# Decoder on one core: the last routed down product in three rounded products, and causal attention's sums transposed between two pairs of pieces

## Chip, cores, metric

One Trainium2 chip, one of its cores, the whole decoder in one launch. The metric is the device time of the execution in microseconds; lower is better. Runs are compared by their median.

## The reference

Four decoder layers over x of 2 x 1024 tokens of 256 values, each with self-attention (or a recurrence), cross-attention to a context of 77 tokens, and a feed-forward, each followed by x = layernorm(x + part(x)). Two parts matter here.

Layer 1's self-attention is causal, with 16 heads of 16 values. Layer 3's feed-forward is routed: 16 experts, 4 per token.

```python
logits = hidden_states @ router_w + router_b
probs = jax.nn.softmax(logits, axis=-1)
topw, topi = jax.lax.top_k(probs, K)                 # K = 4, E = 16
topw = topw / jnp.sum(topw, axis=-1, keepdims=True)
...
hmid = jax.nn.gelu(x @ w1e + b1e, approximate=False) # 256 -> 512
return (acc + (hmid @ w2e + b2e) * ce[:, None], None)  # 512 -> 256
```

## The kernel before

Each engine has its own program, written out by hand; semaphores order them, and every engine works through its own instructions in order. `wait_ge(s, n)` waits until a semaphore has counted to n.

**The routed feed-forward** (`routed_moe`, L2805) is used twice: for layer 1 with a gated unit (`glu`), and last of all for layer 3 without one, which the code calls `biased`. Tokens are sorted by expert into NBLK = 79 blocks of TB = 128 rows. For block j:

- SP (L2930) loads the expert's weights, 1026 KB, into one of WB = 6 buffers `w` as soon as the down product of block j-6 is done. POOL (L2967) gathers the rows into `xb` 6 blocks ahead (`fetch`) and stores the result `yb` to DRAM when it is kept.
- TensorE (L3005): `spin(j)` transposes the rows (L3069), `lift(j)` makes the hidden block in PSUM tiles `A` (8 products of 128x128 by 128 columns, L3082), `drop(j)` the down product in `C` (4 products of 256 columns, L3090). A product of full float32 operands shows as two records in the trace. The order is spin(j+1), lift(j), drop(j-1), and for blocks 2 to 17 also `settle(j-2)` (L3062), gates times bias.
- ACT (L3139): `turn(j+1)` copies the transposed rows (L3155), then four Gelus (L3178) make `hid`. In the last four blocks it also makes the gate diagonals that the final sums need, 8 copies a block (L3195).
- DVE (L3220): `hold(j-1)` copies the down product out of PSUM into `yb` (L3326), and settle's part adds x (L3314).

`C` has two banks. `order` (L2827) deals them out: through drop 16 the drops and the settle products alternate, so that all drops take one bank and drop(j) needs hold(j-1); later the drops alternate and drop(j) needs hold(j-2).

Behind the last block, the results are read back, weighted by the gates, summed, normalised and stored.

**Causal attention** (`stacked_attention`, L1146, `kind` "causal"; the same function with "full" does layer 2). Two things run at once: the row maxima of a later head group, computed in "pieces" that TensorE puts into a ring of 3 PSUM banks (L1491) and DVE reduces (L1632, L1636), and the softmax of the present group: scores `st_ps` (L1483), exponentials on ACT (L1616), and the weighing with the values into the bank `acc` (L1530). When half a group of heads is done ("closing"), DVE transposes the sums from `acc` into `byq` (L1674) and inverts them (L1676); the next half's first weighing waits for `turned`. There are 16 such closings. One step of TensorE is: scores of pair 0 with pieces 2 and 3, weigh (first half of the columns), scores of pair 1 with pieces 0 and 1, weigh (second half, if any), extras. The closing step of a causal half has 128 columns, which all go into the first weigh.

Products in float32r ("rounded") take operands that ACT or DVE has rounded on writing; a float32 value is split into a rounded high part and the rounded rest, and three products (high by high, high by low, low by high) stand for one. The kernel does this already in layer 0's and layer 2's feed-forwards: `hid_hi` L1095, `hid_lo` L1097, `x_hi` and `x_lo` L1071 and L1085, and the products of L2673.

Of the kernel before, what the change touches and what calls it, by code (L numbers as in the profile page):

```python
# [5 lines left out]
F32 = mybir.dt.float32  # L6
F32R = mybir.dt.float32r
# [4 lines left out]
ALU = mybir.AluOpType  # L12
# [3 lines left out]
P = 128  # L16
D = 256
# [1128 lines left out]
def stacked_attention(nc, env, dram, kind, scale, w_count, front, ahead=None):  # L1146
# [86 lines left out]
    with ExitStack() as st:  # L1233
# [3 lines left out]
        with ExitStack() as inner:  # L1237
# [384 lines left out]
            def _(dve):  # L1622
# [55 lines left out]
                def put(step):  # L1678
                    g, half = step // nS, half_of[step % nS]
                    b, u = units[g]  # L1680
                    if u % 2:
                        dve.wait_ge(s.divided, g * HALVES + half + 1)
                        dve.transpose(o[:, u // 2, b * S + half * CH:b * S + (half + 1) * CH], pair[:, half, :]).then_inc(s.evacuated, 1)
# [9 lines left out]
                for step in range(NS + LAG + 3):  # L1693
                    c = step + LEAD if step + LEAD < NC else None
                    if c is not None:
                        pieces(c, (2, 3))
                    if closing(step - LAG - 2):
                        put(step - LAG - 2)
                    if c is not None:
                        pieces(c, (0, 1))  # L1700
                    if closing(step - LAG):
                        turned(step - LAG)
                    if c is not None:
                        extras(c)
# [1100 lines left out]
def routed_moe(nc, env, dram, E, K, F, glu, shared, out=None, ahead=None, front=None, early=None):  # L2805
# [25 lines left out]
    with ExitStack() as st:  # L2831
        z = sbuf(nc, st, "z", [P, NT, D])
        b2 = sbuf(nc, st, "b2", [E, D])
        sc = sbuf(nc, st, "sc", [P, NT, E])
        rowmax = sbuf(nc, st, "rowmax", [P, NT])
        top = sbuf(nc, st, "top", [P, NT, 8])
        topi = sbuf(nc, st, "topi", [P, NT, 8], U32)
        total = sbuf(nc, st, "total", [P, NT])
        g = sbuf(nc, st, "g", [P, NT, K])
        idf = sbuf(nc, st, "idf", [P, NT, K])  # L2840
        eq = sbuf(nc, st, "eq", [P, NT, K, E])
        prod = sbuf(nc, st, "prod", [P, NT, K, E])
        sel = sbuf(nc, st, "sel", [P, E, NT])
        fresh = sbuf(nc, st, "fresh", [P, E, NT])
# [24 lines left out]
        dense = sbuf(nc, st, "dense", [P, NT, E])  # L2869
        gT = sbuf(nc, st, "gT", [E, T])  # L2870
        w = early.w if early else sbuf(nc, st, "w", [P, WB, ROW])
        xb = sbuf(nc, st, "xb", [P, XB, D])
        xbT = sbuf(nc, st, "xbT", [P, 2, KT, TB])
        if front:
            act, hid = (r.rearrange("p a b s -> p (a b s)").rearrange("p (x f n) -> p x f n", x=2, f=NF)
                        for r in (front.parts[:, :, :, :].bitcast(F32), front.plain[:, :, :, :]))
        else:
            act, hid = None, sbuf(nc, st, "hid", [P, 2, NF, TB])
        yb = sbuf(nc, st, "yb", [P, 4, D])
        room = sbuf(nc, st, "room", [P, RU * PAIR * K * D])  # L2880
        stat = sbuf(nc, st, "stat", [P, NT, 6])
        mv = sbuf(nc, st, "mv", [P, NT, 2])
# [8 lines left out]
            for at, n, k in ((0, TB, K), (K * TB, NBLK, K), (K * (TB + NBLK), NBLK, K),  # L2891
# [5 lines left out]
                     "lists_ready owner_ready dense_ready gT_ready gT_kept z_ready z_added s_up s_act s_hid "  # L2897
                     "w0 w1 w2 w3 w4 w5 x0 x1 x2 x3 x4 x5 x6 x7 t_ready t_kept up_ready act_ready "
                     "hid_ready down_done y_kept stored0 stored1 stored2 stored3 got0 got1 got2 got3 got4 got5 got6 got7 "
                     "g_ready scaled blended mixed measured rooted inverted shifted normed spun kept out_stored")  # L2900
        w_ready = (s.w0, s.w1, s.w2, s.w3, s.w4, s.w5)
        x_ready = (s.x0, s.x1, s.x2, s.x3, s.x4, s.x5, s.x6, s.x7)
        stored = (s.stored0, s.stored1, s.stored2, s.stored3)
# [22 lines left out]
        def down_w(src_w, f):  # L2926
            at = NW * KT * F + f * D
            return src_w[:, at:at + D]

        @block.sync  # L2930
        def _(sp):
# [74 lines left out]
        def _(pe):  # L3006
# [65 lines left out]
            def lift(j):  # L3072
# [10 lines left out]
                                           start=(k == 0), stop=(k == KT - 1), skip_group_check=True)  # L3083
                mm.then_inc(s.up_ready, 1)

            def drop(j):
                pe.wait_ge(s.hid_ready, j + 1)
                to = room_c(("drop", j))
                for f in range(NF):
                    mm = pe.matmul(to, hid[:, j % 2, f, 0:TB], down_w(w[:, j % WB], f),  # L3090
                                   start=(f == 0), stop=(f == NF - 1))
                mm.then_inc(s.down_done, 1)
# [47 lines left out]
        def _(act_e):  # L3140
# [16 lines left out]
            def keep(u):  # L3157
                for t in range(u * PAIR, (u + 1) * PAIR):
                    act_e.wait_ge(s.spun, t + 1)
                    act_e.activation(env.xT[:, :, t * P:(t + 1) * P], B[:, t % 2, 0:D].rearrange("p (k n) -> p k n", k=KT), ACT.Copy)\  # L3160
                         .then_inc(s.kept, 1)

            turn(0)
            for j in range(NBLK):
                if j + 1 < NBLK:
# [7 lines left out]
                    act_e.activation(act[:, j % 2, :, 0:TB], A[:, j % 2 * 2, :].rearrange("p (f n) -> p f n", f=NF), ACT.Silu).then_inc(s.act_ready, 1)  # L3173
                else:
                    if j >= 2:
                        act_e.wait_ge(s.down_done, j - 1)
                    for f in range(NF):
                        a = act_e.activation(hid[:, j % 2, f, 0:TB], A[:, j % 2 * 2, f * TB:(f + 1) * TB], ACT.Gelu,  # L3178
                                             bias=w[:, j % WB, NWE + f:NWE + f + 1])
                    a.then_inc(s.hid_ready, 1)  # L3180
                    if j < 2:
                        act_e.wait_ge(s.gT_ready, j + 1)
                        for a in range(2):
                            at = j * (T // 2) + a * CH
                            kept = act_e.activation(gT[:, at:at + CH], A[0:E, 1 + 2 * a, :], ACT.Copy)
                        kept.then_inc(s.gT_kept, 1)
# [34 lines left out]
        def _(dve):  # L3221
# [100 lines left out]
            def hold(j):  # L3322
# [2 lines left out]
                    dve.wait_ge(stored[j % 4], 16 * (j // 4))  # L3325
                dve.tensor_copy(yb[:, j % 4, :], C[:, spot[("drop", j)] % 2, 0:D]).then_inc(s.y_kept, 1)  # L3326

            for j in range(NBLK):
                if glu:
                    dve.wait_ge(s.act_ready, j + 1)  # L3330
                    if j >= 2:
                        dve.wait_ge(s.down_done, j - 1)
                    dve.tensor_tensor(hid[:, j % 2, :, 0:TB], act[:, j % 2, :, 0:TB],  # L3333
                                      A[:, j % 2 * 2 + 1, :].rearrange("p (f n) -> p f n", f=NF), ALU.mult).then_inc(s.hid_ready, 1)
                if j:
                    hold(j - 1)
                    if biased and 0 <= j - 2 < NT:
                        settle(j - 2)
# [311 lines left out]
```

## Time and profile before

| | us |
|---|---|
| median of 3 runs (2590.24 to 2604.8) | 2594.25 |
| the profiled execution's own time | 2600.38 |
| its span, first to last instruction | 2598.6 |
| TensorE products busy, of the span | 2276.5 |
| VectorE busy | 1431.6 |
| ScalarE busy | 1125.8 |
| GpSimd busy | 659.1 |

The mean granted TensorE clock is 0.908 of full speed. PE is TensorE's matmul, PEld its weight load, DVE VectorE, ACT ScalarE, POOL GpSimd, SP the engine that issues most transfers. A row of the timeline merges equal instructions that follow each other; "[0.43 <-PE ring L1491]" is idle time ahead of it and what ended that. Matmuls overlap in the pipeline, so their rate is read from start to start, not from the duration of one.

### The profile page before, as it was taken

Reading aid. Unit: us, or ns where it says so; the run is one execution under the profiler, and the core shown is the slowest. Engines: PE = TensorE matmul, PEld = TensorE weight load, DVE = VectorE, ACT = ScalarE, POOL = GpSimd, SP = SyncE. Lnnn points to the kernel's source line nnn. Section 1 sums busy time; section 2 is a strip of 40 time slices with the busy share of each in tenths; the row PEclk is TensorE's granted clock in tenths of the full one; section 3 lists DMA queues with packets and bytes.
Section 4 is the critical chain, followed back from the end, with each engine's and each line's share of the span. In section 5 each row is a group of like instructions: output and inputs, shape, how many; then the busy total and the mean of one; then the engine's idle time right before and its main releaser. Section 6 shows DMA issues by size and latency. Waiting matters only on the chain. (4 is left out here: it accounts for less than half of the span.)

```text
span 2598.6 us, 41898 instructions
## 1 busy us (share of the span) xinstructions
PE 2276.5 (88%) x15210; PEld 1512.3 (58%) x15210; DVE 1431.6 (55%) x3533; ACT 1125.8 (43%) x1923; POOL 659.1 (25%) x868
## 2 busy tenths in 40 slices
PE   1489999998889999949999998799998798699996
PEld 1387754444436699934444444367665545589995
DVE  6825366785565221158999965666566555511114
ACT  6533335655433011134777774421443334234444
POOL 6110132222110133322011012000356310245551
PEclk8689978988998999966999999789999898699998
DMA  5200122330112189933222101031111210689996
GB/s 195 64 5 1 27 48 46 50 50 18 30 34 106 39 309 334 329 108 54 34 41 35 26 7 46 2 91 58 33 27 19 57 18 2 217 293 354 355 343 235
DMA packets 86208, 268.89 MB, mean 103 GB/s; under 512 B 25306, under 2 KB 43858, under 8 KB 69740
## 3 DMA queue, kind: packets, MB, share of 16 engines
q1 hardware_dynamic: 70324, 233.10, 29.4%
q0 software_dynamic: 15680, 33.12, 4.0%
q8 instruction: 122, 2.00, 0.3%
q14 instruction: 82, 0.67, 0.1%
HBM read 207.36 MB, written 23.94 MB: 89 GB/s over the span
## 5 line engine op out<-in xcount | busy, mean ns | idle before, releaser
L1616 ACT ACTIVATE prob<-st_ps 128x1024 f32<-128x1024 f32 x448 | 412.9, 933 | 220.0 <-PE st_ps L1483 218.7
L1636 DVE TENSOR_REDUCE cmax<-ring 128x1 f32<-128x512 f32 x640 | 401.2, 682 | 43.7 <-PE ring L1491 41.4
L3082 PE MATMUL A<-xbT,w 128*128 128x128 f32 x2512 | 301.3, 276 | 0.3 <-issue 0.3
L3082 PEld LDWEIGHTS A<-xbT,w 128*128 128x128 f32 x2512 | 291.4, 193 | 0.8 <-issue 0.5
L1530 PE MATMUL acc<-prob,v 128*32 128x256 f32 (+2 forms) x3200 | 267.0, 408 | 13.4 <-DVE byq L1674 12.3
L3326 DVE COPY yb<-C 128x256 f32<-128x256 f32 x118 | 50.1, 425 | 283.7 <-PE C L3090 277.5
L2999 POOL DMA_INDIRECT y_rows_dram<-yb,dst x118 | 116.4, 986 | 323.8 <-DVE yb L3326 320.7
L3090 PE MATMUL C<-w,hid 128*128 128x256 f32 x632 | 149.5, 380 | 0.0
L1483 PE MATMUL st_ps<-qst,kst 64*128 64x512 f32 (+3 forms) x560 | 137.3, 489 | 7.3 <-DMA qst<-parts 3.1
L2986 POOL DMA_INDIRECT xb<-x_rows_dram,src x118 | 115.1, 976 | 99.9 <-DVE src L3296 64.6
L1632 DVE CUSTOM_DVE_ANT_0 masked<-ring,causal_wide 128x512 bf16<-128x512 f32 (+3 forms) x256 | 112.5, 487 | 47.8 <-PE ring L1491 46.9
L3178 ACT ACTIVATE hid<-A,w 128x128 f32<-128x128 f32 x316 | 90.3, 369 | 105.6 <-PE A L3082 102.8
L1530 PEld LDWEIGHTS acc<-prob,v 128*32 128x32 f32 x3200 | 65.2, 110 | 120.7 <-issue 104.2
L1491 PE MATMUL ring<-kst,qst 48*128 48x512 f32 (+3 forms) x560 | 127.4, 402 | 2.4 <-DVE cmax L1632 1.8
L1483 PEld LDWEIGHTS st_ps<-qst,kst 64*128 64x128 f32 x560 | 54.9, 192 | 115.3 <-issue 77.9
L3090 PEld LDWEIGHTS C<-w,hid 128*128 128x128 f32 x632 | 114.0, 190 | 12.5 <-ACT hid L3178 0.3
L3155 ACT ACTIVATE xbT<-B 128x256 f32<-128x256 f32 x118 | 45.2, 384 | 171.0 <-PE B L3069 168.6
L1491 PE MATMUL ring<-first 48*128 48x512 f32 (+3 forms) x336 | 106.5, 490 | 10.7 <-PEq L3458 7.4
L2468 ACT ACTIVATE prob<-st_ps 77x1024 f32<-77x1024 f32 x64 | 61.8, 1015 | 124.5 <-PE st_ps L2382 68.0
L2352 PE MATMUL max_ps<-kbd,qT 128*128 128x308 f32 x320 | 109.4, 440 | 5.2 <-DVE negc L2479 3.8
L3333 DVE TENSOR_TENSOR plain<-parts,A 128x512 f32<-128x512 f32 x39 | 26.9, 689 | 155.7 <-ACT parts L3173 155.7
L2479 DVE TENSOR_REDUCE negc<-max_ps 128x4 f32<-128x308 f32 x160 | 76.0, 478 | 60.0 <-PE max_ps L2356 47.2
(475 smaller groups left out, 4491.7 us busy)
## 6 DMA issues: line engine op xcount, KB each, us to landing
w<-L3f_W_dram SPq DMA_DIRECT2D x79, 1026.0 KB
w<-L1f_W_dram SPq DMA_DIRECT2D x39, 1536.0 KB
room<-y_rows_dram SPq DMA_DIRECT2D x8, 1024.0 KB, 10.4
kst<-parts SPq DMA_DIRECT2D x120, 64.0 KB, 2.4
qst<-parts SPq DMA_DIRECT2D x120, 64.0 KB, 2.4
gate<-L2f_gates_dram SPq DMA_DIRECT2D x5, 1536.0 KB, 7.1
first<-parts SPq DMA_DIRECT2D x96, 64.0 KB, 2.4
qT<-dense SPq DMA_DIRECT2D x84, 64.0 KB, 2.4
```

The costliest lines, as they stand in the source:

```text
L1483: mm = pe.matmul(st_ps[:, p, side, 0:hi - lo], stack_of(1, g)[rows, p, j * P:(j + 1) * P], stack_of(0, g)[rows, p, lo:hi], start=True, sto ...
L1491: pe.matmul(spot(key)[:, 0:k1 - k0], stack_of(0, gm)[rows, 1 - p, t * P:(t + 1) * P], stack_of(1, gm)[rows, 1 - p, k0:k1], start=True, sto ...
L1530: mm = pe.matmul(acc[32 * a:32 * (a + 1), lo - half * CH + c0:lo - half * CH + c1], v[:, g // 2 % 2, j, units[g][1] % 2 * HU + a, :], prob ...
L1616: act.activation(prob[:, step % PROBS, 2 * p:2 * p + 2, 0:n], st_ps[:, p, :, 0:n], ACT.Exp, scale=scale)\
L1632: dve.tensor_tensor_reduce(out=masked[:, a, 0:k1 - k0], in0=spot(key)[:, 0:k1 - k0], in1=env.causal_wide[:, CH - (k1 - k0):], scale=1.0, s ...
L1636: dve.tensor_reduce(cmax[:, a, t:t + 1, k0 // CH], spot(key)[:, 0:k1 - k0], AX.X, ALU.max)\
L2352: mm = pe.matmul(to, qT[:, g % SLOTS, t * P:(t + 1) * P], kbd[:, u, b].rearrange("p a m -> p (a m)"), start=True, stop=(not masked), skip_ ...
L2986: pool.indirect_dma_start(out=xb[:, j % XB, :], out_offset=None, in_=rows[:, :], in_offset=bass.IndirectOffsetOnAxis(ap=src[:, j:j + 1], a ...
L2999: pool.indirect_dma_start(out=yk, out_offset=bass.IndirectOffsetOnAxis(ap=dst[:, j:j + 1], axis=0), in_=yb[:, j % 4, :], in_offset=None).t ...
L3082: mm = pe.matmul(A[:, j % 2 * 2 + a, f * TB:(f + 1) * TB], up_w(w[:, j % WB], a, k, f), xbT[:, j % 2, k, :], start=(k == 0), stop=(k == KT ...
L3090: mm = pe.matmul(to, hid[:, j % 2, f, 0:TB], down_w(w[:, j % WB], f), start=(f == 0), stop=(f == NF - 1))
L3178: a = act_e.activation(hid[:, j % 2, f, 0:TB], A[:, j % 2 * 2, f * TB:(f + 1) * TB], ACT.Gelu, bias=w[:, j % WB, NWE + f:NWE + f + 1])
```

## The change

In `stacked_attention`, for causal attention alone, DVE does `turned` (wait for the closing weigh, transpose, reciprocal) between the pieces 2, 3 and the pieces 0, 1 of a step, instead of behind both.

In `routed_moe`, for the last feed-forward alone: ACT rounds each block's down weights (`raise_down`, once ahead of the loop and then behind the Gelus of the block before); DVE subtracts to get their low part (`lower_down`) and splits the hidden block (`part_hid`), ahead of `hold`; `drop` becomes 12 rounded products. Its Gelu waits for the split of block j-2, no longer for its drop. To make room for the four new buffers, `sc` and `eq` are laid into `env.wide`, and `xb`, `yb` and `hid` into `env.xT`.

```diff
                     if closing(step - LAG - 2):
                         put(step - LAG - 2)
+                    if kind == "causal" and closing(step - LAG):
+                        turned(step - LAG)
                     if c is not None:
                         pieces(c, (0, 1))
-                    if closing(step - LAG):
+                    if kind == "full" and closing(step - LAG):
                         turned(step - LAG)
...
+            def drop_in_parts(j):
+                pe.wait_ge(s.down_low, j + 1)
+                pe.wait_ge(s.hid_low, j + 1)
+                to = room_c(("drop", j))
+                for f in range(NF):
+                    cols = slice(f * D, (f + 1) * D)
+                    pe.matmul(to, hid_hi[:, j % 2, f, :], down_hi[:, j % 2, cols], start=(f == 0), stop=False)
+                    pe.matmul(to, hid_hi[:, j % 2, f, :], down_lo[:, j % 2, cols], start=False, stop=False)
+                    mm = pe.matmul(to, hid_lo[:, j % 2, f, :], down_hi[:, j % 2, cols], start=False, stop=(f == NF - 1))
+                mm.then_inc(s.down_done, 1)
+
             def drop(j):
+                if biased:
+                    drop_in_parts(j)
+                    return
                 pe.wait_ge(s.hid_ready, j + 1)
...
+            def raise_down(j):
+                act_e.wait_ge(w_ready[j % WB], 16 * (j // WB + 1))
+                if j >= 2:
+                    act_e.wait_ge(s.down_done, j - 1)
+                act_e.activation(down_hi[:, j % 2, :], down_rows(j), ACT.Copy).then_inc(s.down_high, 1)
+
+            if biased:
+                raise_down(0)
             turn(0)
...
                     if j >= 2:
-                        act_e.wait_ge(s.down_done, j - 1)
+                        act_e.wait_ge(s.hid_low, j - 1)
                     for f in range(NF):
                         a = act_e.activation(hid[:, j % 2, f, 0:TB], A[:, j % 2 * 2, f * TB:(f + 1) * TB], ACT.Gelu,
                                              bias=w[:, j % WB, NWE + f:NWE + f + 1])
                     a.then_inc(s.hid_ready, 1)
+                    if j + 1 < NBLK:
+                        raise_down(j + 1)
...
+            def lower_down(j):
+                dve.wait_ge(s.down_high, j + 1)
+                dve.tensor_tensor(down_lo[:, j % 2, :], down_rows(j), down_hi[:, j % 2, :].bitcast(F32), ALU.subtract).then_inc(s.down_low, 1)
+
+            def part_hid(j):
+                dve.wait_ge(s.hid_ready, j + 1)
+                if j >= 2:
+                    dve.wait_ge(s.down_done, j - 1)
+                dve.tensor_copy(hid_hi[:, j % 2], hid[:, j % 2]).then_inc(s.hid_high, 1)
+                dve.wait_ge(s.hid_high, j + 1)
+                dve.tensor_tensor(hid_lo[:, j % 2], hid[:, j % 2], hid_hi[:, j % 2].bitcast(F32), ALU.subtract).then_inc(s.hid_low, 1)
+
+            if biased:
+                lower_down(0)
             for j in range(NBLK):
+                if biased:
+                    part_hid(j)
+                    if j + 1 < NBLK:
+                        lower_down(j + 1)
```

## Rows read from the trace of the kernel before

**Rows 1.** Stretches: us, busy us of PE, PEld, DVE, ACT, POOL, granted clock, DMA share, GB/s

```profile
2230.00:2240.00 10.00, 9.93 (x63) 8.49 (x61) 7.22 (x9) 0.00 (x0) 0.00 (x0) 0.50 0.99 411
2262.00:2322.00 60.00, 60.00 (x372) 49.15 (x371) 11.04 (x26) 21.01 (x69) 25.68 (x27) 1.00 0.88 294
2340.00:2530.00 190.00, 190.00 (x1325) 176.97 (x1323) 21.65 (x51) 77.91 (x255) 99.48 (x102) 1.00 0.96 351
```

**Rows 2.** The timeline, one block (start us, us, engine, line, operation, count)

```profile
2402.37 1.95 PE L3082 MATMUL A<-xbT,w 128*128 128x128 f32 x16
...
2404.15 1.89 PE L3090 MATMUL C<-w,hid 128*128 128x256 f32 x8
...
2404.36 1.15 ACT L3178 ACTIVATE hid<-A,w 128x128 f32<-128x128 f32 x4 [1.40 <-PE A L3082]
...
2405.88 0.38 PE L3069 MATMUL B<-ident,xb 128*128 128x128 f32 x2
...
2406.09 0.42 DVE L3326 COPY yb<-C 128x256 f32<-128x256 f32 x1 [3.31 <-PE C L3090]
2406.10 1.95 PE L3082 MATMUL A<-xbT,w 128*128 128x128 f32 x16
2406.30 0.38 ACT L3155 ACTIVATE xbT<-B 128x256 f32<-128x256 f32 x1 [0.80 <-PE B L3069]
```

**Rows 3.** The timeline of TensorE, two drops among the early blocks

```profile
2270.84 1.89 PE L3090 MATMUL C<-w,hid 128*128 128x256 f32 x8
...
2275.35 1.89 PE L3090 MATMUL C<-w,hid 128*128 128x256 f32 x8
```

**Rows 4.** The waits in causal attention: us in total, times, longest

```profile
PE acc L1530 <- DVE byq L1674: 1.6, 4, 0.4
```

**Rows 5.** The timeline of TensorE, the first and last of nine rounded products, dense feed-forward

```profile
1724.12 0.39 PE L2673 MATMUL hid_ps<-x_hi,w_hi 128*128 128x512 f32 x1
...
1725.99 0.40 PE L2673 MATMUL hid_ps<-x_hi,w_lo 128*128 128x512 f32 x1
```

**Rows 6.** The timeline, pairs of half-height rounded products, 256 and 512 columns

```profile
478.53 0.39 PE L1483 MATMUL st_ps<-first 64*128 64x256 f32 x2
...
478.75 0.53 PE L1491 MATMUL ring<-kst,qst 48*128 48x512 f32 x2
...
530.31 0.50 PE L1483 MATMUL st_ps<-qst,kst 64*128 64x512 f32 x2
530.65 0.79 PE L1491 MATMUL ring<-kst,qst 48*128 48x512 f32 x2
```

**Rows 7.** The groups of instructions by line before 340 us (busy us, mean ns | idle before)

```profile
L1097 DVE TENSOR_TENSOR hid_lo<-lift,hid_hi 128x512 fp32r<-128x512 f32 x32 | 22.1, 692 | 1.1
...
L1095 DVE CAST hid_hi<-lift 128x512 fp32r<-128x512 f32 x32 | 13.7, 429 | 10.1 <-ACT lift L1077 10.1
...
L1085 DVE TENSOR_TENSOR first<-xT,parts 128x1024 fp32r<-128x1024 f32 x4 | 4.6, 1221 | 6.0 <-ACT parts L1071 6.0
...
L1071 ACT ACTIVATE parts<-xT 128x1024 fp32r<-128x1024 f32 x4 | 3.9, 1045 | 1.3 <-PEq L3423 1.3
```

**Rows 8.** The timeline, the last four blocks

```profile
2542.52 1.14 ACT L3178 ACTIVATE hid<-A,w 128x128 f32<-128x128 f32 x4 [1.40 <-PE A L3082]
...
2544.31 2.45 ACT L3195 ACTIVATE w<-ident,g 128x128 f32<-128x128 f32 x8 [0.65 <-PE C L3090]
...
2553.30 3.75 PE L3090 MATMUL C<-w,hid 128*128 128x256 f32 x16
```

**Rows 9.** The timeline, one closing in causal attention

```profile
477.55 0.43 PE L1530 MATMUL acc<-prob,v 128*32 128x128 f32 x8
...
478.44 0.29 DVE L1632 CUSTOM_DVE_ANT_0 masked<-ring,causal_wide 128x128 bf16<-128x128 f32 x1 [0.43 <-PE ring L1491]
...
478.87 0.71 DVE L1674 STREAM_TRANSPOSE byq<-acc 128x512 f32<-128x512 f32 x1
...
479.73 0.64 PE L1530 MATMUL acc<-prob,v 128*32 128x256 f32 x8 [0.44 <-DVE byq L1674]
```

More of the change, by code:

```diff
@@ L2833, in routed_moe @@
         b2 = sbuf(nc, st, "b2", [E, D])
-        sc = sbuf(nc, st, "sc", [P, NT, E])
+        sc = env.wide[:, 4 * KT * P:4 * KT * P + NT * E].rearrange("p (t e) -> p t e", t=NT) if biased else sbuf(nc, st, "sc", [P, NT, E])
         rowmax = sbuf(nc, st, "rowmax", [P, NT])
@@ L2840, in routed_moe @@
         idf = sbuf(nc, st, "idf", [P, NT, K])
-        eq = sbuf(nc, st, "eq", [P, NT, K, E])
+        eq = env.wide[:, 0:NT * K * E].rearrange("p (t k e) -> p t k e", t=NT, k=K) if biased else sbuf(nc, st, "eq", [P, NT, K, E])
         prod = sbuf(nc, st, "prod", [P, NT, K, E])
@@ L2871, in routed_moe @@
         w = early.w if early else sbuf(nc, st, "w", [P, WB, ROW])
-        xb = sbuf(nc, st, "xb", [P, XB, D])
+        flat_xT = env.xT[:, :, :].rearrange("p k t -> p (k t)")
+        xb = flat_xT[:, 0:XB * D].rearrange("p (x d) -> p x d", x=XB) if biased else sbuf(nc, st, "xb", [P, XB, D])
         xbT = sbuf(nc, st, "xbT", [P, 2, KT, TB])
@@ L2877, in routed_moe @@
         else:
-            act, hid = None, sbuf(nc, st, "hid", [P, 2, NF, TB])
-        yb = sbuf(nc, st, "yb", [P, 4, D])
+            act, hid = None, flat_xT[:, (XB + 4) * D:(XB + 4) * D + 2 * NF * TB].rearrange("p (x f n) -> p x f n", x=2, f=NF)
+            hid_hi = sbuf(nc, st, "hid_hi", [P, 2, NF, TB], F32R)
+            hid_lo = sbuf(nc, st, "hid_lo", [P, 2, NF, TB], F32R)
+            down_hi = sbuf(nc, st, "down_hi", [P, 2, NF * D], F32R)
+            down_lo = sbuf(nc, st, "down_lo", [P, 2, NF * D], F32R)
+        yb = flat_xT[:, XB * D:(XB + 4) * D].rearrange("p (x d) -> p x d", x=4) if biased else sbuf(nc, st, "yb", [P, 4, D])
         room = sbuf(nc, st, "room", [P, RU * PAIR * K * D])
@@ L2899, in routed_moe @@
                      "hid_ready down_done y_kept stored0 stored1 stored2 stored3 got0 got1 got2 got3 got4 got5 got6 got7 "
-                     "g_ready scaled blended mixed measured rooted inverted shifted normed spun kept out_stored")
+                     "down_high down_low hid_high hid_low g_ready scaled blended mixed measured rooted inverted shifted normed spun kept out_stored")
         w_ready = (s.w0, s.w1, s.w2, s.w3, s.w4, s.w5)
@@ L2928, in down_w, with down_rows @@
             return src_w[:, at:at + D]
+        def down_rows(j):
+            return w[:, j % WB, NW * KT * F:NWE]
         @block.sync
```

## The prediction

> **What bounds the kernel now.** I read the busy time by stretch first, then one block of the last stage in the timeline, then the same for the causal closings. The last stage, the routed feed-forward with 79 blocks, takes the last 350 us but the final sums. In it TensorE has no idle time at the 2.4 GHz level (granted clock 1.00), once 190 us long at 351 GB/s and a DMA share of 0.96 [rows 1]. The timeline of a block shows why: lift, down product ("drop") and transposes ("spin") follow each other without a gap, lift 2402.37 to 2404.15 = 1.78 us, drop to 2405.88 = 1.73, spin to 2406.10 = 0.22, together 3.73 us, while ACT waits for the lift and DVE for the drop [rows 2]. In the blocks up to about 17, which also have a gate-times-bias product, the period is 2275.35 - 2270.84 = 4.51 us [rows 3]. So TensorE sets this stage, and the DMA queues have little left. In causal attention a head group closes 16 times; the next accumulation there waits for the transpose of the sums only 1.6 us in all, 4 times [rows 4].
>
> **The drop.** It loses 4 full products (8 records, 1.73 us) and gets 12 rounded ones of 256 columns. The trace has none of that shape with all 128 rows. Nearest: nine rounded products of 512 columns start between 1724.12 and 1725.99, 1.87 / 8 = 0.234 us apart, each with a weight load of its own [rows 5]; by column that is 0.457 ns, so 0.117 us for 256. The pairs of half-height rounded products take 0.22 us for 256 columns and 0.34 for 512 [rows 6]: 0.12 more for 256 more columns, so the same rate, on a base of 0.10 us that looks like an exposed weight load. Lower bound 0.111: lift's 16 records, which move two passes of 128 columns and load 128 weight columns each, take 1.78 us [rows 2]. Upper bound 0.22. I take 0.117, because the full-height row is nearest in form: 12 x 0.117 = 1.40 us, 0.33 less. TensorE's block would then be 3.40 us.
>
> The Trainium skill (TensorE: Matmul & The Clock Gate, Part 3, The mechanism) says that a weight load overlaps running matmuls only when its row group differs, which would put a full-height product at load plus stream. By that rule the drop would take 12 x 0.22 = 2.6 us; the full-height rows disagree, as 16 loads and 16 products fit in 1.78 us [rows 2].
>
> **What ACT and DVE get.** Per block ACT rounds the down weights, 128x1024: 1.05 us by the like copy; DVE subtracts them, 1.22, rounds the hidden block, 0.43, and subtracts, 0.69 [rows 7]. ACT has then 0.38 + 1.15 + 1.05 = 2.58 us a block and DVE 1.22 + 0.43 + 0.69 + 0.42 = 2.76, both under 3.40 [rows 2, 7]. The order matters. Gelu starts with the end of lift(j) and takes 1.15; the two hidden parts are ready 1.15 + 0.43 + 0.69 = 2.3 us behind it, 2.4 with handovers; drop(j) comes only after drop(j-1), spin and lift(j+1), 1.40 + 0.22 + 1.78 = 3.4 us. Hidden, with 1.0 us to spare; without that cover the drop would wait by the difference.
>
> The copy-out of drop(j-1) now stands on DVE behind the parts of block j and the low weights of block j+1, and those wait for ACT, which waits for drop(j-1). From the start of drop(j-1): 1.40 + 0.17 (its last product's tail: 2404.15 + 1.89 against 2405.88) + 1.05 + 1.22 + 0.42, with four handovers of some 0.04, 4.4 us. Up to block 17 the drops share one PSUM bank, so drop(j) waits for just this copy: period 4.4, not 4.51 - 0.33 = 4.18. Gain 17 x 0.1 = 2 us. Behind, two banks alternate and the wait has a period to spare. The gathers and stores on POOL move later by some 2.3 us but run 6 blocks ahead and 4 buffers deep; the weights of block j+6 are issued by SP at the same event as before, the end of drop(j). The rounding of block j+1 waits on ACT for that block's transfer and for drop(j-1), with turn(j+2) queued behind it; lift(j+1) needs the same transfer and turn(j+2) is wanted a block later: nothing. Moving xb, yb, hid, sc and eq into other memory adds no instruction; nothing else of the last stage uses that memory.
>
> **DMA.** At 351 GB/s a 3.73 us block moves 1.31 MB. The engines' time per block is share times period: 0.96 x 3.73 = 3.58 us; in the slower early blocks it is 0.88 x 4.51 = 3.97 [rows 1, 3]. It falls by half of what the period falls; carried on, it meets the period at 3.43, and if it falls no more, at 3.58. A block between 3.40 and 3.58: I take the middle, 3.49, 0.24 less than now, over the 58 blocks from 17 to 75: 14 us. What is late then is the weight transfer in flight.
>
> **The end.** In the last four blocks ACT also makes the gate diagonals, 2.45 us each. With the weights' rounding its turn is 0.38 + 1.15 + 1.05 + 2.45 = 5.03 us, above 3.4, so it sets the pace. From the first of these Gelus at 2542.52 to the last product's end at 2553.30 + 3.75 the trace has 14.5 us [rows 8]. New: three ACT turns of 5.03, 0.4 in which the first rounding waits for drop(74), less 0.38 for the turn that the last lacks, Gelu 1.15, parts 1.12, handovers, drop 1.40 + 0.17: 19.1 us. Loss 4.6. The first weights' rounding lies under the wait for the lists: nothing.
>
> **Causal closings.** The closing step's weighing ends at 477.55 + 0.43 = 477.98, ahead of the pieces for which DVE waits 0.43 us until 478.44; the transpose starts only at 478.87, and the product that needs it at 479.73 after 0.44 us [rows 9]. Moved, the transpose (0.71) and the small reciprocal run from 478.0 to about 479.0, and the two pieces follow 0.5 us later than before; their ring places come free later, and TensorE's next pieces wait. Each event lies between 0.44 won and 0.5 lost: over 16, -7 to +8 us. As DVE's idle 0.43 is used but the ring takes most of it back, I take 1 us won.
>
> **Sum.** 14 + 2 - 4.6 + 1 = 12.4 us. The profiled execution (2598.6 us of span, 2600.4 in all) would be 2588. It is 6 us above the median of the three runs, 2594.25, and of that I forecast 2582.
>
> **Rivals.**
> - DMA keeps its pace. The 351 GB/s over 190 us may be the ceiling of this mix of weights, gathers and stores; then a block stays at 3.73 and the end still costs: 0 + 2 - 4.6 + 1, 2 us lost, 2596. For: share 0.96. Against: weight transfers alone ran at 411 GB/s [rows 1]. The Trainium skill (DMA: Bandwidth & Descriptors, Specifications) puts HBM's limit for one core at about 358 GB/s, which is 1.31 / 358 = 3.66 us a block and 2592 for the whole; the 411 GB/s disagree.
> - Weight loads exposed, the slow side. As in the pairs [rows 6], each rounded product costs 0.22: drop 2.64, 0.91 more than now. 58 x 0.91, 17 blocks of 3.0 + 2.64 against 4.51 (19 us), the end at 4.6 + 1.2, less 1: 77 us, 2671. It decides early: at 0.136 a product the gain is gone, at 0.15 the kernel is over 0.5% slower. For: the 0.10 us base in the pairs. Against: the full-height rows [rows 5].
> - TensorE alone sets the block. DMA follows to 3.40: 19 + 2 - 4.6 + 1 = 17 us, 2577; with the closings at their best 2571.
> - The closings turn bad: the pieces' ring stalls TensorE at every closing, 8 us back, 2591. DVE's wait on the sums then stands in front of work that had been ready.
>
> **How the numbers follow.** Measured against the median, 0.5% (13 us) is about what can be told from no change. Forecast 0.38, with its block between 3.43 and 3.58 (2579 to 2587); TensorE alone 0.29; DMA's pace 0.14; closings bad 0.08; exposed loads 0.11. Faster by over 0.5%: TensorE alone and two fifths of the forecast, 0.44. Slower: exposed loads and a little for causal attention, 0.13. The same: 0.43. The range goes from 2569, closings won besides, to 2602, closings bad with DMA at its pace and a few us between runs; beyond it lie the exposed loads.
>
> **What would show it.** Right: 12 down records 0.117 us apart at full clock; blocks of about 3.5 us with a DMA share near 1.0 and lift waiting on the weights' transfer now and then; 4.4 us before block 17 with drop waiting for yb; ACT without a gap in the last four blocks, the drops there waiting for hid_lo; in causal attention the transposes about 0.9 us earlier, DVE's gap ahead of the pieces gone. Wrong: products 0.15 apart or more; a steady block above 3.65 or below 3.35; idle before the drops in the middle of the stage, which would mean that the ACT and DVE chain is longer than summed; or causal attention changed by more than 8 us.

## The result, and the profile after

Over 20 runs each, the kernel before takes 2594.3 us (2588.9 to 2604.8) and the changed one 2581.4 (2572.1 to 2587.7): ratio 0.9952, 95% interval 0.9942 to 0.9961. That is 12.9 us between the medians, and 0.48% by the ratio. The forecast was 2582. The profiled execution takes 2583.9 us (span 2582.2), against 2600.4 before.

The stretches of the last stage in the trace after (columns as in [rows 1]):

```profile
2310.00:2340.00 30.00, 29.53 (x238) 27.63 (x238) 20.55 (x34) 19.05 (x47) 15.21 (x15) 1.00 0.85 308
2340.00:2510.00 170.00, 168.81 (x1473) 168.60 (x1472) 131.76 (x198) 121.26 (x295) 137.71 (x98) 1.00 0.96 378
```

TensorE is still busy all the time but for 1.2 us. The transfers' share is 0.96 as before, but they move 378 GB/s, not 351. DVE was busy for 11% of the time before and is at 78%; POOL was at 52% and is at 81%. The timeline of one steady block after, which answers to [rows 2]:

```profile
2402.36 1.23 DVE L3364 TENSOR_TENSOR down_lo<-w,down_hi 128x1024 fp32r<-128x1024 f32 x1 [0.18 <-issue]
2402.63 1.81 POOL L2996 DMA_INDIRECT xT<-x_rows_dram,src  x1 [0.30 <-issue]
...
2402.94 0.36 PE L3102 MATMUL C<-down_hi,hid_hi 128*128 128x256 f32 x1
...
2403.14 0.28 PE L3103 MATMUL C<-down_lo,hid_hi 128*128 128x256 f32 x1
...
2403.26 0.28 PE L3104 MATMUL C<-down_hi,hid_lo 128*128 128x256 f32 x1
...
2403.32 1.14 ACT L3210 ACTIVATE xT<-A,w 128x128 f32<-128x128 f32 x4 [0.72 <-PE A L3092]
...
2404.34 0.28 PE L3104 MATMUL C<-down_hi,hid_lo 128*128 128x256 f32 x1
...
2404.45 0.38 PE L3079 MATMUL B<-ident,xT 128*128 128x128 f32 x2
2404.50 0.43 DVE L3370 CAST hid_hi<-xT 128x512 fp32r<-128x512 f32 x1 [0.57 <-ACT xT L3210]
...
2404.67 1.73 PE L3092 MATMUL A<-xbT,w 128*128 128x128 f32 x14
2404.71 1.06 ACT L3191 ACTIVATE down_hi<-w 128x1024 fp32r<-128x1024 f32 x1 [0.25 <-PE C L3104]
2404.74 1.05 POOL L3009 DMA_INDIRECT y_rows_dram<-xT,dst  x1 [0.30 <-issue]
...
2404.96 0.69 DVE L3372 TENSOR_TENSOR hid_lo<-xT,hid_hi 128x512 fp32r<-128x512 f32 x1
```

(The hidden block and the gathered rows now lie in `xT`.) The drop, from its first product to the first transpose, is 2404.45 - 2402.94 = 1.51 us, the spin 0.22, and the lift (to the next drop, 2406.38 in the block after) 1.71: together 3.44 us, which is the period of the lifts in 55 of the 57 blocks from the 18th to the 75th; it was 3.73.

I summed the last stage in three executions of each kind: the kernel before, once more (e12 below) and with the turned move alone (e1); the changed kernel, once more (e11) and with the drop alone (e2). Starts of lifts, us:

| stretch | before, e12, e1 | after, e11, e2 | mean difference |
|---|---|---|---|
| first 18 blocks | 80.95, 80.66, 82.11 | 82.14, 81.43, 82.24 | +0.7 |
| lift 18 to lift 75 | 212.85, 213.28, 213.04 | 197.82, 198.12, 197.78 | -15.2 |
| lift 75 to the end of the kernel | 58.04, 58.43, 58.53 | 62.57, 62.91, 62.75 | +4.4 |
| together | 351.8, 352.4, 353.7 | 342.5, 342.5, 342.8 | -10.0 |

In the first row the first block alone scatters from 3.9 to 5.3 us in both kernels. From lift 1 to lift 18 it is 76.8 us in all three traces without the rounded drop, and 76.9, 77.3 and 76.9 with it: 0.3 lost, not 0.7.

So the last stage gives 10.0 us, just short of the 10.1 to 15 that the timing allows. In the two profiled executions another 7.1 us lie ahead of it (first lift at 2239.6, before at 2246.7). That is scatter: over all 14 profiles the first lift begins between 2230.6 and 2246.7, and the changed kernel itself has 2239.6 and 2230.6. The differences grow in steps of 1 to 3 us in stages that nobody touched, and also between the two executions of the kernel before (2246.7 and 2237.1). For one part of the kernel, compare its own length, not the positions in two traces.

### The profile page after: what moved, and what is told of

Same layout as the page of the kernel before. It is cut to its first block and busy times, and to the rows that moved or that the text cites. A ratio compares the mean times of both kernels' runs of the same rounds, so it can differ in the third digit from the quotient of the medians.

```text
span 2582.2 us, 43002 instructions
## 1 busy us (share of the span) xinstructions
PE 2254.6 (87%) x15526; PEld 1515.0 (59%) x15526; DVE 1604.8 (62%) x3770; ACT 1199.7 (46%) x2002; POOL 702.1 (27%) x868
## 5 line engine op out<-in xcount | busy, mean ns | idle before, releaser
L1530 PE MATMUL acc<-prob,v 128*32 128x256 f32 (+2 forms) x3200 | 266.4, 407 | 11.4 <-DVE byq L1674 10.7
L2996 POOL DMA_INDIRECT xT<-x_rows_dram,src x79 | 117.2, 1483 | 53.1 <-DVE src L3330 29.3
L3210 ACT ACTIVATE xT<-A,w 128x128 f32<-128x128 f32 x316 | 90.1, 368 | 66.0 <-PE A L3092 66.0
L3364 DVE TENSOR_TENSOR down_lo<-w,down_hi 128x1024 fp32r<-128x1024 f32 x79 | 96.8, 1225 | 20.0 <-issue 10.5
L3009 POOL DMA_INDIRECT y_rows_dram<-xT,dst x79 | 84.7, 1072 | 81.7 <-DVE xT L3360 63.9
L3191 ACT ACTIVATE down_hi<-w 128x1024 fp32r<-128x1024 f32 x79 | 83.7, 1059 | 45.8 <-PE C L3104 26.7
L1919 POOL TENSOR_SCALAR_AFFINE_SELECT prob<-prob 128x512 f32<-128x512 f32 (+1 forms) x136 | 80.9, 596 | 76.3 <-ACT prob L2100 69.1
L3102 PE MATMUL C<-down_hi,hid_hi 128*128 128x256 f32 x316 | 96.1, 304 | 4.7 <-DVE hid_lo L3372 2.6
```

What stands on the lines that cost most here:

```text
L1530: mm = pe.matmul(acc[32 * a:32 * (a + 1), lo - half * CH + c0:lo - half * CH + c1], v[:, g // 2 % 2, j, units[g][1] % 2 * HU + a, :], prob ...
L2996: pool.indirect_dma_start(out=xb[:, j % XB, :], out_offset=None, in_=rows[:, :], in_offset=bass.IndirectOffsetOnAxis(ap=src[:, j:j + 1], a ...
L3102: pe.matmul(to, hid_hi[:, j % 2, f, :], down_hi[:, j % 2, cols], start=(f == 0), stop=False)
L3364: dve.tensor_tensor(down_lo[:, j % 2, :], down_rows(j), down_hi[:, j % 2, :].bitcast(F32), ALU.subtract).then_inc(s.down_low, 1)
```

## Experiments

All were timed against the kernel before on the same chip; ratios are to it.

**e1: the turned move alone.** The kernel before with this:

```diff
+                    if kind == "causal" and closing(step - LAG):
+                        turned(step - LAG)
                     if c is not None:
                         pieces(c, (0, 1))
-                    if closing(step - LAG):
+                    if kind == "full" and closing(step - LAG):
                         turned(step - LAG)
```

> The kernel before with the turned move in causal attention alone. The forecast gave this part 1 us (range 7 us won to 8 us lost), the rival of bad closings 8 us lost. The trace of after has causal attention within 1 us of before (start of the first masked reduction 2.0 us later, of the last 2.4 us later), but the last stage begins 7.1 us earlier. If the move wins those 7 us, this run is about 7 us faster than before (ratio 0.997); if the 7 us is scatter between executions, it is within 2 us of it (ratio 0.999 to 1.001).

2592.2 against 2595.1 us, ratio 0.9995 (0.998 to 1.0009): nothing that can be told. Its last stage began at 2233.5 us, 13 us sooner than in the trace of before, with medians 3 us apart: scatter again.

Why nothing? The waits in causal attention from 333 to 613 us, first of the kernel before, then of the changed one (us in total, times, longest):

```profile
DVE masked L1632 <- PE ring L1491: 46.9, 66, 2.6
...
PEld ring L1491 <- DVE cmax L1632: 12.8, 34, 0.6
DVE cmax L1636 <- PE ring L1491: 11.6, 24, 1.1
```

```profile
DVE masked L1632 <- PE ring L1491: 40.1, 54, 2.8
...
PEld ring L1491 <- DVE cmax L1632: 15.4, 39, 0.6
DVE cmax L1636 <- PE ring L1491: 14.4, 31, 1.2
```

In these rows DVE waits 4 us less in all, and TensorE's loads 2.6 us more for the ring banks. One pair of traces says little, so I also added up all waits of weight loads for ring banks, over the whole stage in each of the 14 traces: 36.4 to 36.8 us in the three without the move, 38.0 to 39.0 in the eleven with it. TensorE waits about 2 us more for the ring, and the 1.6 to 1.9 us for `byq` are gone. DVE's waits for the ring overlap (60.7 to 64.1 us without, 58.1 to 60.9 with). The closing of [rows 9] shows it singly. In the timeline after:

```profile
479.20 0.43 PE L1530 MATMUL acc<-prob,v 128*32 128x128 f32 x8
...
479.69 0.72 DVE L1674 STREAM_TRANSPOSE byq<-acc 128x512 f32<-128x512 f32 x1
...
480.92 0.18 PEld L1491 LDWEIGHTS ring<-kst,qst 48*128 48x128 f32 x1 [0.44 <-DVE cmax L1632]
...
481.35 0.64 PE L1530 MATMUL acc<-prob,v 128*32 128x256 f32 x8
```

From the closing weighing the transpose now starts 0.49 us on, not 1.32; the next weighing starts 2.15 us on, not 2.18. The 0.44 us that TensorE waited for `byq` its weight load now waits, ahead of the pieces, for a ring bank. The stage from the first masked reduction to the last takes 281.5, 280.5 and 278.0 us without the move (before, e12, e2) and 278.4 to 281.9 in eleven executions with it.

**e2: the drop alone.** The changed kernel with that edit undone.

> The changed kernel with causal attention as before, so the rounded down product alone. The period of the lifts should again be 3.44 us in the steady blocks and 4.56 in the first 17. If the whole gain is the last stage's, the ratio is that of the changed kernel, 0.995; if the turned move carries 7 us of it, 0.998.

2582.2 us, ratio 0.9945 (0.9925 to 0.9965), blocks of 4.56 and 3.44. The whole gain is the drop's.

**e3: eight products.** The changed kernel without the products of the hidden block's low part, so the result lacks that term:

```diff
-                    pe.matmul(to, hid_hi[:, j % 2, f, :], down_lo[:, j % 2, cols], start=False, stop=False)
-                    mm = pe.matmul(to, hid_lo[:, j % 2, f, :], down_hi[:, j % 2, cols], start=False, stop=(f == NF - 1))
+                    mm = pe.matmul(to, hid_hi[:, j % 2, f, :], down_lo[:, j % 2, cols], start=False, stop=(f == NF - 1))
```

> The changed kernel without the products of the hidden block's low part (that term is left out of the result), so 8 instead of 12 products in a drop; ACT, DVE, POOL and the transfers do what they did. If TensorE alone sets the block of 3.44 us, it falls by 4 x 0.117 to 2.97. If the transfers have a ceiling, it stays above: 1.30 MB at the 411 GB/s of the weights alone is 3.17 us, and a ceiling at what after has (378 GB/s) leaves 3.44. If POOL sets it (gather 1.79, store 1.05 and two gaps of 0.30 fill its 3.44 us), 3.44 too, or 2.9 or less if its gathers shorten. ACT's 2.6 and DVE's 2.8 us lie below.

2560.9 us in two runs, 0.9864 (0.9831 to 0.9897). Some blocks take 2.96 us, the first ones and those behind a long one; the 57 from 18 to 75 average 183.35 / 57 = 3.22. The steady stretch of e3:

```profile
2325.00:2495.00 170.00, 166.04 (x1388) 158.62 (x1386) 140.80 (x214) 128.14 (x322) 134.90 (x108) 1.00 1.01 408
```

and its waits there:

```profile
POOL y_rows_dram L3009 <- issue: 16.7, 52, 1.2
POOL xT L2996 <- issue: 15.9, 52, 0.3
PEld A L3092 <- DMA w<-L3f_W_dram: 6.7, 25, 0.8
PEld B L3079 <- DMA xT<-x_rows_dram,src: 4.2, 8, 1.3
```

I read this as the transfers' ceiling: 408 GB/s at a share of 1.01, with TensorE waiting for weights 25 times, and the weights landing 12.7 us after their request (8.8 in e4 between 2340 and 2510); 3.22 us x 408 GB/s = 1.31 MB a block. It is the 411 GB/s of the weights alone [rows 1], for the mix with gathers and stores. The changed kernel at 3.44 us is 0.22 above it, so TensorE sets its block. At 2.96 the transfers would be too slow. And 0.48 for four products is 0.12 each once more. POOL does not set the 3.44 us either, since the block falls to 3.22 and below.

But e3 shows a second engine without slack. POOL is busy for 134.9 of the 170 us and spends another 32.6 in the pauses of some 0.30 us between its instructions: 167.5 together. TensorE also waits for gathered rows, 8 times. Whether a faster transfer alone would bring 2.96 us is not shown; POOL might hold the block then.

**e7: the rounding without its products.** The changed kernel with the four full products back, and all the new work of ACT and DVE kept:

```diff
-                for f in range(NF):
-                    cols = slice(f * D, (f + 1) * D)
-                    pe.matmul(to, hid_hi[:, j % 2, f, :], down_hi[:, j % 2, cols], start=(f == 0), stop=False)
...
+                for f in range(NF):
+                    mm = pe.matmul(to, hid[:, j % 2, f, 0:TB], down_w(w[:, j % WB], f), start=(f == 0), stop=(f == NF - 1))
```

> The changed kernel with all the rounding work of ACT and DVE kept, but the down product in the four full products of before. If the rounding is hidden in the steady blocks, their period is that of before, 3.73 us, and TensorE has no idle time there. In the first 17 the chain rounding, subtraction, copy-out, drop should give 4.56 + 0.22 = 4.8 us against 4.51 before, and the end 4.6 us more: about 9 us slower than before, ratio 1.0035. If the rounding were not hidden, the steady blocks would show idle time ahead of the drops and a period above 3.75.

2600.3 us, ratio 1.0031 (1.0019 to 1.0042): 8 us slower than before. The steady blocks keep 3.73 us, so the rounding there is hidden; the early ones take 4.86 instead of 4.51, and from lift 75 to the end it takes 61.97 instead of 58.3. By its trace, the last stage and what follows take 363.3 us: the rounding costs 363.3 - 352.6 = 10.7, and the products win 363.3 - 342.6 = 20.7 back. Half of what TensorE gains is given away, and 9.7 of the 10.7 us in the first 18 blocks (6.0) and from lift 75 on (3.7); the other 1.0 is mostly two longer blocks, 4.08 and 4.58 us.

**e4: the copy-out first.** DVE's loop of the changed kernel:

```diff
                 if biased:
                     part_hid(j)
+                    if j:
+                        hold(j - 1)
                     if j + 1 < NBLK:
                         lower_down(j + 1)
...
-                if j:
+                if j and not biased:
                     hold(j - 1)
-                    if biased and 0 <= j - 2 < NT:
-                        settle(j - 2)
+                if biased and 0 <= j - 2 < NT:
+                    settle(j - 2)
```

> The changed kernel with the copy-out of the previous drop ahead of the low weights of the next block on DVE. My theory: the first 17 blocks take 4.56 us by the chain rounding on ACT, subtraction and copy-out on DVE, drop; with the copy-out first, TensorE sets them: 4.51 less the 0.29 that the drop lost, 4.22; 15 x 0.34 = 5 us faster than the changed kernel, ratio to before 0.993. Rival: the gate-times-bias product or its sum sets them, and they stay at 4.5, ratio 0.995. The steady blocks stay at 3.44 in both.

2572.1 us, 0.9911 (0.989 to 0.9932). The early blocks fall to 4.20 us. So the chain it was. In the timeline of the changed kernel an early block reads:

```profile
2273.68 0.19 PEld L3102 LDWEIGHTS C<-down_hi,hid_hi 128*128 128x128 f32 x1 [0.28 <-issue]
...
2275.09 0.28 PE L3104 MATMUL C<-down_hi,hid_lo 128*128 128x256 f32 x1
...
2275.46 1.06 ACT L3191 ACTIVATE down_hi<-w 128x1024 fp32r<-128x1024 f32 x1 [0.69 <-PE C L3104]
...
2276.55 1.23 DVE L3364 TENSOR_TENSOR down_lo<-w,down_hi 128x1024 fp32r<-128x1024 f32 x1 [0.60 <-issue]
...
2277.70 0.42 DVE L3360 COPY xT<-C 128x256 f32<-128x256 f32 x1
...
2278.23 0.19 PEld L3102 LDWEIGHTS C<-down_hi,hid_hi 128*128 128x128 f32 x1 [0.28 <-issue]
```

Drop to rounding 1.78, rounding to subtraction 1.09, to the copy 1.15, to the next drop 0.53: 4.55. The stretch from the first lift to the end falls from 342.6 to 333.9 us, 8.7: 5.8 in the early blocks, 1.8 between lift 18 and lift 75, mostly because a stall of 1.4 us in the middle is gone, the rest at the end. That stall, one block of 4.85 us whose lift starts at 2459.7, is a late gather (at 2463 TensorE waited 1.2 us for `xT` from `x_rows_dram`). In the trace of before the same gather is 1.4 us late too, behind a store that POOL began 2.87 us after its last work ended, and nobody waits for it. What holds that store is not shown.

**e5: half of the diagonals on POOL.** On top of e4, ACT makes diagonals 0 and 1 of each tile, and POOL makes 2 and 3, ahead of its stores of the last four blocks:

```diff
+                        for k in range(K // 2, K):
+                            a = pool.tensor_scalar(diag[:, n, k, :], env.ident[:, :], g[:, tile, k:k + 1], None, ALU.mult)
```

> The copy-out-first kernel (e4_hold_first) with half of the gate diagonals of the last four blocks on POOL, ahead of its stores, instead of on ACT. Theory: ACT's turn of 0.38 + 1.14 + 1.06 + 2.46 = 5.04 us sets the last blocks; with 1.23 less it is 3.8, the last lifts are 3.8 us apart or less, not 4.6, and 3 to 4 us are won against e4_hold_first: about 2568.5. Rival: the diagonals on POOL (it shows no such operation in this stage) delay the stores that the closing loads wait for, and the time stays at 2572 or rises.

2578.0 us, 0.9935 (0.9923 to 0.9947): 6 slower than e4 by the ratios, though the two intervals touch; from the first lift to the end it has 336.1 us against 333.9. Nothing was won, as the rival said. The last two lifts come 3.45 and 3.21 us behind the ones ahead, as hoped, after one of 4.71, but:

```profile
2532.86 0.42 DVE L3372 COPY xT<-C 128x256 f32<-128x256 f32 x1 [1.47 <-PE C L3114]
...
2534.84 2.34 POOL L3016 TENSOR_SCALAR w<-ident,g 128x128 f32<-128x128 f32 x4
...
2537.35 1.01 POOL L3019 DMA_INDIRECT y_rows_dram<-xT,dst  x1 [0.17 <-issue]
```

A diagonal costs POOL 2.34 / 4 = 0.59 us (ACT 0.31), and 0.66 to 0.90 beside DVE's subtractions (2.65 and 3.60 us for the four of the blocks before); the last store starts at 2537.35, though its rows were kept by 2532.86 + 0.42. All that follows the last block waits for it.

**e6: the subtraction in two.** On top of e4, `down_lo` in two instructions of 512 columns:

```diff
+                for half in range(2):
+                    cols = slice(half * NF // 2 * D, (half + 1) * NF // 2 * D)
+                    d = dve.tensor_tensor(down_lo[:, j % 2, cols], down_rows(j)[:, cols], down_hi[:, j % 2, cols].bitcast(F32), ALU.subtract)
```

> The copy-out-first kernel with the 1.22 us subtraction of the low down weights in two instructions of half the columns (some 0.7 us each). Theory: an indirect transfer's instruction on POOL waits for the DVE instruction that is running when it starts, and takes 0.86 us from that one's end; its stores, which start 0.35 us into the subtraction, then fall from 1.73 to about 1.2 us (first half ends 0.34 us behind their start). Rival: the load on memory or the transfers stretch them, and they stay at 1.73. The time stays that of e4_hold_first, 2572, in both, since the block is TensorE's.

2571.9 us in two runs, 0.9916 (0.9898 to 0.9933), as e4. The stores take 1.20 us. First e4, then e6:

```profile
2402.20 1.22 DVE L3364 TENSOR_TENSOR down_lo<-w,down_hi 128x1024 fp32r<-128x1024 f32 x1
2402.55 1.74 POOL L3009 DMA_INDIRECT y_rows_dram<-xT,dst  x1 [0.43 <-DVE xT L3360]
```

```profile
2405.66 1.29 DVE L3366 TENSOR_TENSOR down_lo<-w,down_hi 128x512 fp32r<-128x512 f32 x2
2406.02 1.20 POOL L3009 DMA_INDIRECT y_rows_dram<-xT,dst  x1 [0.97 <-DVE xT L3360]
```

**e8 and e9: the diagonals behind the last Gelu**, on top of e4, and on the changed kernel alone:

```diff
-                    part = j - (NBLK - 4)
-                    if part >= 0:
+                    for part in range(4 if j == NBLK - 1 else 0):
```

> The copy-out-first kernel (e4_hold_first) with all 32 gate diagonals behind the last block's Gelu on ACT, not spread over the last four blocks. Theory: ACT's turn there is then 2.6 us, so the last lifts keep 3.44 us (e4: 3.81 and 4.57) and the last drop waits only for the last block's own Gelu and parts, some 4 us earlier; the diagonals (32 x 0.31 = 9.9 us) run while the last stores land and the closing loads come in, 11 us in which ACT and TensorE wait. 3 to 4 us faster than e4_hold_first, about 2568, ratio to before 0.990. Rival: the diagonals end behind the loads and the closing products wait for them: the time stays at 2572.

> The changed kernel with the diagonals behind the last Gelu and nothing else, so the copy-out where the change has it. If the end's 4.6 us are ACT's turn of 5.04 us, 3 to 4 us faster than the changed kernel, about 2578, ratio to before 0.994; the early blocks stay at 4.56. If the end is held by something else (stores, the chain of drops), it stays at 2581.

e8: 2572.5 us, 0.9910 (0.9891 to 0.9928), no better than e4. e9: 2577.1, 0.9933 (0.9913 to 0.9954), about 4 under the changed kernel, which the interval can't tell; from the first lift to the end e9 has 339.8 us, 2.8 less. The end alone, from lift 75, won 3.5 us there (59.2 against 62.7), as expected; the middle lost 1.3. In e8 the rival that I had named did not come about either: the closing products wait 11.1 us for their loads, and the diagonals are done before. Another wait took the place of the one removed:

```profile
ACT down_hi L3191 <- DMA w<-L3f_W_dram: 3.2, 2, 2.8
PEld A L3092 <- DMA w<-L3f_W_dram: 3.1, 2, 2.5
```

The weights took 7 to 9 us from request to landing around 2350 to 2400 us, and 13 to 17 at the end (12 to 14 in the kernel before too, where nobody waits for them); why they take longer there is not shown. The blocks up to lift 75 lost 3.5 us against e4 and the end won 2. One caution: this trace is of e8's longest execution, 2578.1 us, where the other five took 2570.2 to 2574.6, so these waits may be longer than usual.

**e10: the weights sooner.** On top of e8:

```diff
-                if j >= WB:
+                if biased and j >= WB:
+                    sp.wait_ge(s.down_low, j - WB + 1)
+                    sp.wait_ge(s.hid_ready, j - WB + 1)
+                elif j >= WB:
                     sp.wait_ge(s.down_done, j - WB + 1)
```

> e8_diag_last with the weights of block j+6 requested as soon as block j's own are used up (low down weights made and hidden block ready), no longer at the end of drop(j), 3.8 us later; the drop no longer reads them. In e8_diag_last the weights took 8 to 9 us to land in the middle of the stage and 13 to 17 at its end, and the last lifts waited 2.5 us twice for them. Theory: with 3.8 us more in hand these waits shrink, the last lifts come near 3.44 us, and the 4 us that e8_diag_last missed appear: about 2568, ratio to before 0.990. Rival: the transfers are at their ceiling there, a sooner request only queues longer, and the time stays at 2572.

2569.1 us, ratio 0.9906 (0.9885 to 0.9927), the fastest of the kernels here that compute everything (e3 leaves a term out), 26 us under the kernel before. Its last blocks keep 3.44 and 3.22 us, no wait for weights is left, and from the first lift to the end it has 331.0 us, against 335.5 in e8 and 333.9 in e4. The timed ratios alone don't separate it from e4 or e8, and each trace is one execution.

**e11 and e12: both kernels once more.**

> The changed kernel once more, to tell what of the 7 us by which its last stage began sooner is scatter: the start of the last stage may lie anywhere from 2233 to 2247, as in the other runs; the last stage itself, from the first lift to the last, takes 291.8 us again, within 1.

> The kernel before once more. From the first lift to the end of the execution it had 351.8 us, with the turned move alone 353.7; the changed kernel has 342.5, 342.8 and 342.5 in three executions, 9.3 to 11 less, while the medians of the timed runs differ by 12.9 (10 to 15). If that stretch of the kernel before takes 352 to 356 us again, the last stage accounts for the whole gain within what the timing can tell; if it is 351.8 to the tenth, some 3 us of the gain lie ahead of it. The start of the first lift may lie anywhere from 2231 to 2247.

e11: 2582.6 us, 0.9957 (0.994 to 0.9975), first lift at 2230.6, first lift to last 292.2. e12: 2595.9, 1.0001 (0.9982 to 1.002), first lift at 2237.1, from there to the end 352.4. As expected, but that e11's last stage began 2.4 us below the range that I had named. By e11's own interval the gain is 6.5 to 15.6 us, and 10.0 lies within. The 2.9 us between 10.0 and 12.9 are not shown anywhere; the scatter ahead of the last stage is wide enough to hold them.

## Why the prediction was right, and where it was not

The total (2582 against 2581.4) is better than its terms: -14, -2, +4.6, -1 were forecast, together -12.4; -15.2, +0.7, +4.4 and 0 were measured in the traces, together -10.1. That the forecast came within 1 us of the median is luck: it leans on the 2.9 us that no stage shows.

- **The drop**, right. I took 0.117 us a product from the full-height row [rows 5]; the steady block shows 0.12 (2403.14, 2403.26, ... 2404.34). The first product of a drop stands 0.20 apart from the second, so the drop takes 1.51, not 1.40; the lift takes 1.71 instead of 1.78. My 3.40 us for TensorE was 0.04 short. The weight loads are not exposed: twelve of 0.19 us lie beside twelve products in 1.5 us. The Trainium skill (TensorE: Matmul & The Clock Gate, Part 3, The mechanism) has a sentence by which a load of the same row group does not overlap running products. It does not hold for these products: the trace disagrees, 0.12 against 0.22. The same section also says that a load into the background weight buffer is pulled ahead, which I had left out; whether these loads go there, no run shows. The rival that priced exposed loads from the half-height pairs is out too.
- **DMA**, wrong. The failed step is the extrapolation of the DMA engines' time per block ("share times period"), which was to fall "by half of what the period falls". Measured: 0.96 x 3.44 = 3.30 after, 0.96 x 3.73 = 3.58 before: it fell by 0.28, all of what the period fell. The busy share is not the work: one weight packet (8 KB) took 382 ns on average at 294 GB/s, 347 at 351, 321 at 378 and 320 at 408, with a median of 311 to 314 in all four stretches. So the packets were longer where less was moved, and the share stays at 0.96 from 351 to 378 GB/s; why, is not shown. What holds is the rate: 1.31 MB at 408 to 411 GB/s, 3.2 us. The middle of my bounds, 3.49, was 0.05 too high; the rival "TensorE alone" described the steady blocks. And the lifts never waited for weights there. 57 blocks at 0.294 are 16.8; the 1.4 us stall and the block of 3.79 us at lift 18 leave about 15.
- **Early blocks**, the mechanism right, the sign wrong. The chain ran as written, but at 4.56, not 4.42: its first term, drop to rounding, is 1.78 instead of 1.40 + 0.17 + 0.04. Of the other terms, the copy starts 1.15 us behind the subtraction, not 1.26, and the drop 0.53 behind the copy, not 0.46. Against 4.51 before, 0.14 us a block turned 2 us won into 0.7 lost by the table, 0.3 of it clear of the first block's scatter. I had seen this chain, priced it, and overlooked that an order with nothing in front of the copy-out was free to be had: 6 us.
- **The end**, right in sum. From the first of the last four Gelus (2521.57) to the end of the last product (2540.24 + 0.41) it is 19.1 us, as forecast. But the last Gelu came 13.9 us after the first, not 15.1. The turns are 5.06, 4.55 and 4.29 us from Gelu to Gelu, where the forecast had 5.43, 5.03 and 4.65: ACT's instructions that follow without a wait start about 0.1 us before the one ahead has ended (2526.63 + 1.11 against 2527.63), at each of the four joints of a turn, and I had added full durations. And the last drop's products start 0.215 us apart, not 0.12: behind 2.63 us without work TensorE's granted clock was 0.53 of full speed, about the 1.2 GHz level. In e8, behind 1.09 us without work, the last drop's products start 0.12 apart. That the sum is right is luck: the two errors, 1.2 us each, cancel. The timeline, and the stretch with the clock in its third last column:

```profile
2521.57 1.14 ACT L3210 ACTIVATE xT<-A,w 128x128 f32<-128x128 f32 x4 [0.62 <-PE A L3092]
...
2526.63 1.11 ACT L3210 ACTIVATE xT<-A,w 128x128 f32<-128x128 f32 x4
...
2527.63 1.06 ACT L3191 ACTIVATE down_hi<-w 128x1024 fp32r<-128x1024 f32 x1
...
2531.18 1.12 ACT L3210 ACTIVATE xT<-A,w 128x128 f32<-128x128 f32 x4
...
2535.47 1.14 ACT L3210 ACTIVATE xT<-A,w 128x128 f32<-128x128 f32 x4
...
2537.89 0.41 PE L3102 MATMUL C<-down_hi,hid_hi 128*128 128x256 f32 x1 [2.63 <-DVE hid_lo L3372]
2538.10 0.41 PE L3103 MATMUL C<-down_lo,hid_hi 128*128 128x256 f32 x1
...
2540.24 0.41 PE L3104 MATMUL C<-down_hi,hid_lo 128*128 128x256 f32 x1
```

```profile
2537.90:2540.60 2.70, 2.70 (x12) 2.46 (x12) 0.23 (x1) 2.33 (x5) 0.96 (x1) 0.53 0.16 55
```

- **Causal closings**, right: "the ring takes most of it back" is what the waits of all 14 traces show, and it takes all.
- **Cover**, right. ACT and DVE fit: the hidden block's parts are done at 2404.96 + 0.69 = 2405.65, 0.7 us ahead of the drop that needs them. What I did not foresee is POOL, whose gathers and stores get longer, and the late gather that costs 1.4 us at 2463; I had put POOL at nothing.

## What to carry over

When an engine's work is made shorter, the new work on its neighbours is free only where its whole chain is shorter than the period: list the blocks that are different (the first with an extra product, the last with extra scaling) and sum the chain for those, then order each engine's queue so that what frees a bank stands first. Read a transfer limit from bytes over the best rate seen, not from the busy share. And a relief at one place shows the next wait: here ACT's turn, then the weights' request, each worth 2 to 4 us by the traces, which the timed runs alone can't tell.

## What was not expected

**POOL waits for DVE.** The gathers on POOL took 0.97 us in nearly every block of the kernel before and up to 1.89 in the changed one, whose POOL is busy or between two instructions for the whole 3.44 us (gather 1.79, store 1.05, twice 0.30). One rule fits: if a DVE cast or subtraction is already running when an indirect transfer's instruction starts on POOL, the latter ends 0.86 us after that DVE instruction; else it takes 0.97 to 0.99. In the changed kernel 153 of its 158 gathers and stores lie within 0.05 us of this, in e4 155. In the rows of e4 above: 2402.20 + 1.22 + 0.86 = 2404.28, and the store ends at 2404.29. In e6 the first half ends about 0.69 us after 2405.66, and 0.86 later is 2407.21; the store ends at 2407.22. Where POOL's instruction starts within some 0.05 us of DVE's, it is not lengthened. The Trainium skill (GPSIMD Engine Reference, 8. Key points) says that GpSimd shares its SBUF interfaces with VectorE and contends with DVE instructions in a two-port mode or with two inputs in SBUF; the subtractions are of the second kind, and these rows agree. The cast has one input; whether it runs in a two-port mode no run here shows. It cost no time here, because the block is TensorE's: in e2 the gathers between 2337 and 2450 keep 0.97 and the block is 3.44 us too.

**A high transfer share is not a limit.** A share of 0.96 stood beside 351, 376 and 378 GB/s; only at 408 did TensorE wait for weights throughout the stretch.
